# Inverse norms of queries and keys on the GpSimd engine with its power operation, and each sine product as one VectorE operation: a 12-layer local-attention and feed-forward kernel

## The reference

```python
def l2norm(t):
    return t / jnp.maximum(jnp.linalg.norm(t, axis=-1, keepdims=True), 1e-12)

def rotate_half(x):
    x1, x2 = jnp.split(x, 2, -1)
    return jnp.concatenate([-x2, x1], -1)

def attn_layer(x, Wqkv, qs, ksc, Wo):          # 16 heads of 64
    ...
    q = l2norm(q) * qs
    k = l2norm(k) * ksc
    ...
    q = q * cos * scale + rotate_half(q) * sin * scale
    k = k * cos * inv + rotate_half(k) * sin * inv
    out = local_attention(q, k, v)
    ...
    return out @ Wo
```

## Time and profile before

| | |
|---|---|
| median of 3 runs | 7130.14 us (7125.9 to 7132.31) |
| the profiled execution | 7134.42 us, span 7132.6 us |
| busy share of the span | DVE 85%, PE 83%, PEld 54%, ACT 46%, POOL 34% |
| granted TensorE clock, mean | 0.934 of full speed |
| first stack, from its first tiles to its end | about 418 to 2700 us |
| top-k attention between the stacks | about 2700 to 4800 us |
| one layer of a stack (exponential of tile 0 to the same of the next layer) | 354.8 us (958.07 to 1312.91) |
| one full tile step | 17.3 us |

### The profile page before, as it was taken

How to read it: one execution, slowest core, us unless ns; L and a number is a source line. 1 busy time by engine, 2 the same in 40 slices (tenths; PEclk the granted TensorE clock), 3 DMA queues, 4 the chain that set the end, 5 groups by cost and what they waited for, 6 DMA issues and landing times. The chain is left out here.

```text
span 7132.6 us, 149904 instructions
## 1 busy us (share of the span) xinstructions
PE 5922.3 (83%) x47404; PEld 3834.3 (54%) x47596; DVE 6041.5 (85%) x12676; ACT 3310.3 (46%) x6408; POOL 2418.6 (34%) x1391
## 2 busy tenths in 40 slices
PE   5776888888888887988988988986888888888888
PEld 2224545555555554565565566565555555555555
DVE  5988888888888885998998998996979797979797
ACT  3335656565555552222222222222656565656564
POOL 1444444434343431122122122221525253525252
PEclk7998999999999998998998998988999999999999
DMA  0002222222222210000000000000212121212121
GB/s 14 0 0 63 59 52 59 52 59 52 59 52 59 53 46 14 1 1 1 1 1 1 1 1 1 1 1 15 60 51 60 51 60 51 61 50 62 50 62 37
DMA packets 159611, 244.33 MB, mean 34 GB/s; under 512 B 36597, under 2 KB 57009, under 8 KB 157495
## 3 DMA queue, kind: packets, MB, share of 16 engines
q1 hardware_dynamic: 159158, 238.71, 13.3%
HBM read 36.20 MB, written 1.05 MB: 5 GB/s over the span
## 5 line engine op out<-in xcount | busy, mean ns | idle before, releaser
L879 POOL TENSOR_TENSOR f_rope<-f_rope,f_t 128x1024 f32<-128x1024 f32 x384 | 907.3, 2363 | 1551.9 <-DVE f_t L759 1551.9
L1315 PE MATMUL psum<-tk_kT,tk_qs 128*128 128x512 f32 (+3 forms) x4128 | 1262.4, 466 | 9.1 <-POOL tk_qs L1548 9.1
L1548 POOL TENSOR_TENSOR tk_qs<-tk_qT,tk_mix 128x1024 f32<-128x1024 f32 x258 | 497.8, 1932 | 1588.6 <-PE psum L1316 1423.9
L882 POOL TENSOR_TENSOR f_rope<-f_rope,f_rn 128x1024 f32<-128x1024 f32 x384 | 752.6, 1960 | 721.1 <-DVE f_rn L738 706.1
L1315 PEld LDWEIGHTS psum<-tk_kT,tk_qs 128*128 128x128 f32 x4128 | 756.8, 208 | 439.7 <-issue 297.6
L454 PE MATMUL psum<-f_wqkv,f_xs 128*128 128x512 f32 x1536 | 774.1, 610 | 84.9 <-DMA f_wqkv<-in_Wqkv 56.0
L1505 DVE MAX8 tk_m<-tk_work 128x8 f32<-128x528 f32 (+3 forms) x1792 | 818.6, 496 | 2.3 <-issue 1.2
L1511 DVE MATCH_REPLACE8 tk_work<-tk_m,tk_work 128x400 f32<-128x400 f32 (+3 forms) x1536 | 743.8, 491 | 0.5
L755 DVE TENSOR_TENSOR f_rope<-f_raw,f_rot 128x1024 f32<-128x1024 f32 x384 | 627.2, 1633 | 24.5 <-ACT f_raw L600 17.6
L600 ACT ACTIVATE f_raw<-psum 128x512 f32<-128x512 f32 x768 | 454.6, 595 | 247.3 <-PE psum L454 187.9
L473 PEld LDWEIGHTS psum<-ident,f_rope 128*128 128x128 f32 x3072 | 350.4, 144 | 343.9 <-ACT f_qT L600 216.5
(11 more groups left out here) (234 smaller groups left out, 10915.4 us busy)
## 6 DMA issues: line engine op xcount, KB each, us to landing
f_v<-f_v_tok SPq DMA_DIRECT2D x1152, 128.0 KB, 2.4
f_v<-f_v_tok SPq DMA_DIRECT2D x768, 64.0 KB, 2.0
f_wqkv<-in_Wqkv SPq DMA_DIRECT2D x12, 1536.0 KB, 6.6
f_wo<-in_Wo SPq DMA_DIRECT2D x12, 512.0 KB, 4.0
f_w<-in_W SPq DMA_DIRECT2D x12, 341.0 KB
f_w<-in_W SPq DMA_DIRECT2D x24, 64.0 KB
tk_wkv<-in_Wkv SPq DMA_DIRECT2D x1, 1024.0 KB, 6.0
out<-y_tok SPq DMA_DIRECT2D x4, 256.0 KB, 2.5
```

Source lines behind the costliest of these rows:

```text
L879: pool.tensor_tensor(part, part, t2[:, half, :, :], ALU.add).then_inc(s["rope_added"], 1)
L882: pool.tensor_tensor(part, part, rn[:, H * half:H * (half + 1)].unsqueeze(2).to_broadcast([P, H, DH]), ALU.mult).then_inc(s["add_done"], 1)
L1315: pe.matmul(psum[:, j, 0:n], qs[:, j, c, :], kT[:, c, 0:n], start=(c == 0), stop=False, skip_group_check=True)
L1548: pool.tensor_tensor(qs[:, j, :, :], qT[:, :, P * t:P * (t + 1)], mix[:, :, heads(p, j)].to_broadcast([P, PAIRS, P]), ALU.mult).then_inc(s ...
```

## The change

- `newton` and the table `magic` are gone from DVE. A function `inverse_norm` on POOL makes `rn` in six operations on 128x32 elements: the maximum with 1e-24, the power -0.5 (`ALU.pow`, with a tile that holds -0.5), and one polishing step of four operations. It is placed between the sum (L879, now L872) and the multiplication (L882, now L877) of half 0, and waits for both reductions of the tile.
- DVE's sum and reciprocal of the softmax follow the reductions directly. Before the first reduction DVE waits for the inverse norms of the tile before (`rn_ready`).
- The two sine operations of a half become one of 1024 columns, which reads `raw` through a view with the two halves of each head in reversed order.

```diff
@@ -714,31 +713,6 @@
                 for sem, n in ((s["rot_done"], 2), (s["ss_done"], 2), (s["sub_done"], 1), (s["on_done"], 1)):
                     dve.sem_inc(sem, n)
 
-                def newton(g, between):
-
-                    at = [0]
-
-                    def link(ins):
-                        at[0] += 1
-                        ins.then_inc(s["newton"], 1)
-                        if at[0] in between:
-                            between[at[0]]()
-
-                        wait_alone(dve, s["newton"], NEWTON * g + at[0], s["scrap"]) if at[0] == 2 else dve.wait_ge(s["newton"], 1 + NEWTON * g + at[0])
-
-                    x, h, y, z = (nt[:, n, :] for n in range(4))
-                    link(dve.tensor_scalar(x, ss[:, :], 1e-24, None, ALU.max))
-                    link(dve.tensor_scalar(h.bitcast(U32), x.bitcast(U32), 1, 0xFFFFFFFF, ALU.logical_shift_right, ALU.bitwise_xor))
-                    link(dve.tensor_tensor(y.bitcast(U32), h.bitcast(U32), k.magic[:, :], ALU.add))
-                    for n in range(3):
-                        link(dve.scalar_tensor_tensor(z, y, -0.5, y, ALU.mult, ALU.mult))
-                        link(dve.tensor_tensor(h, z, x, ALU.mult))
-                        if n == 2:
-                            dve.wait_ge(s["add_done"], 1 + 2 * g + 2)
-                            dve.scalar_tensor_tensor(rn[:, :], h, 1.5, y, ALU.add, ALU.mult).then_inc(s["rn_ready"], 1)
-                        else:
-                            link(dve.scalar_tensor_tensor(y, h, 1.5, y, ALU.add, ALU.mult))
-
                 def shifted(L, b, j, t):
 
                     late = not isinstance(t, int) or t >= 2
@@ -754,10 +728,10 @@
                     cos = rot[:, half, j, :].unsqueeze(1).to_broadcast([P, H, DH])
                     dve.tensor_tensor(rope[:, j % 2, half, :, :], raw[:, half, :, :], cos, ALU.mult)
                     dve.wait_ge(s["add_done"], 1 + 2 * g + half + 1)
-                    for q in range(2):
-                        sin = rot[:, 2 + half, j, hd * q:hd * (q + 1)].unsqueeze(1).to_broadcast([P, H, hd])
-                        last = dve.tensor_tensor(t2[:, half, :, hd * q:hd * (q + 1)], raw[:, half, :, hd * (1 - q):hd * (2 - q)], sin, ALU.mult)
-                    last.then_inc(s["rot_done"], 1)
+                    sin = rot[:, 2 + half, j, :].rearrange("p (q e) -> p q e", q=2).unsqueeze(1).to_broadcast([P, H, 2, hd])
+                    swapped = raw[:, half, :, :].rearrange("p h (q e) -> p h q e", q=2)[:, :, ::-1, :]
+                    dve.tensor_tensor(t2[:, half, :, :].rearrange("p h (q e) -> p h q e", q=2), swapped, sin,
+                                      ALU.mult).then_inc(s["rot_done"], 1)
 
                 def step(L, b, j, kk):
                     g0 = LT * L + kk
@@ -784,10 +758,10 @@
                         rotate(g0, j, 0)
                         for half in range(2):
                             dve.wait_ge(s["sq_done"], 1 + 2 * g0 + half + 1)
+                            if half == 0:
+                                dve.wait_ge(s["rn_ready"], 1 + g0)
                             dve.tensor_reduce(ss[:, H * half:H * (half + 1)], sq[:, half, :, :], AX_X, ALU.add).then_inc(s["ss_done"], 1)
-                        dve.wait_ge(s["ss_done"], 1 + 2 * g0 + 2 + 2)
-                        newton(g0, {2: den_sum, 4: den_recip} if on(kk, 2) else {})
-                    elif on(kk, 2):
+                    if on(kk, 2):
                         den_sum()
                         den_recip()
                     if on(kk, 2):
@@ -860,6 +834,25 @@
 
             @block.gpsimd
             def _(pool):
+                def inverse_norm(g):
+
+                    x, y, z, h = (nt[:, n, :] for n in range(4))
+                    n0 = 1 + NEWTON * g
+                    wait_alone(pool, s["ss_done"], 2 * g + 2 + 2, s["scrap"])
+                    pool.tensor_scalar(x, ss[:, :], 1e-24, None, ALU.max).then_inc(s["newton"], 1)
+                    pool.wait_ge(s["newton"], n0 + 1)
+                    pool.tensor_tensor(y, x, minus_half[:, :], ALU.pow).then_inc(s["newton"], 1)
+                    pool.wait_ge(s["newton"], n0 + 2)
+                    pool.tensor_tensor(z, y, y, ALU.mult).then_inc(s["newton"], 1)
+                    pool.wait_ge(s["newton"], n0 + 3)
+                    pool.tensor_tensor(h, z, x, ALU.mult).then_inc(s["newton"], 1)
+                    wait_alone(pool, s["newton"], NEWTON * g + 4, s["scrap"])
+                    pool.tensor_scalar(z, h, -0.5, 1.5, ALU.mult, ALU.add).then_inc(s["newton"], 1)
+                    pool.wait_ge(s["newton"], n0 + 5)
+                    pool.tensor_tensor(rn[:, :], y, z, ALU.mult).then_inc(s["rn_ready"], 1)
+
+                pool.memset(minus_half[:, :], -0.5).then_inc(s["halved"], 1)
+                pool.wait_ge(s["halved"], 1 + 1)
                 pool.sem_inc(s["wo_done"], 1)
                 pool.sem_inc(s["out_full"], 1)
                 pool.sem_inc(s["add_done"], 2)
@@ -877,6 +870,8 @@
                             pool.wait_ge(s["rot_done"], 1 + 2 * g0 + half + 1 + 2)
                             part = rope[:, j % 2, half, :, :]
                             pool.tensor_tensor(part, part, t2[:, half, :, :], ALU.add).then_inc(s["rope_added"], 1)
+                            if half == 0:
+                                inverse_norm(g0)
                             pool.wait_ge(s["rope_added"], 1 + 2 * g0 + half + 1)
                             pool.wait_ge(s["rn_ready"], 1 + g0 + 1)
                             pool.tensor_tensor(part, part, rn[:, H * half:H * (half + 1)].unsqueeze(2).to_broadcast([P, H, DH]),
```

More of the change, by code:

```diff
@@ L36 @@
 REMOVED = -3.4e38
-MAGIC = 0x5F3759DF
-NEWTON = 11
+NEWTON = 5
 HCH = [(0, 128), (128, 128), (256, 85)]
@@ L249, in _ @@
             dve.memset(k.XB[:, :, :], 0.0)
-            dve.memset(k.magic[:, :], MAGIC + 1)
             dve.wait_ge(s["built"], 1 + 1)
@@ L337, in ffn_stack @@
         s = names(ctx, phase, nc, *LN_SEMS, "wqkv_in", "wo_in", "w12_in", "tabled", "zeroed", "xs_ready", "proj_full", "proj_evac", "v_in_even", "v_in_odd",
-                  "sq_done", "ss_done", "newton", "rn_ready", "rope_added", "rot_done", "add_done", "t_full",
+                  "sq_done", "ss_done", "newton", "halved", "rn_ready", "rope_added", "rot_done", "add_done", "t_full",
                   "t_evac", "scores", "top", "sub_done", "exp_done", "summed", "rden_done", "pv_done", "on_done",
@@ L355, in ffn_stack @@
         rn = sb("rn", [P, 2 * H])
+        minus_half = sb("minus_half", [P, 2 * H])
         rope = sb("rope", [P, 2, 2, H, DH])
@@ L1587, in build @@
         k.mask_f, k.causal, k.band = sb("mask_f", [P, P]), sb("causal", [P, P], BF16), sb("band", [P, 2, 8, 2 * WIN], BF16)
-        k.eps, k.one, k.magic = sb("eps", [P, 1]), sb("one", [P, 1]), sb("magic", [P, 2 * H], U32)
+        k.eps, k.one = sb("eps", [P, 1]), sb("one", [P, 1])
         k.b1, k.b2 = sb("b1", [P, DEPTH, 2, 3]), sb("b2", [P, DEPTH])
```

## The result

The changed kernel takes 7308.56 us (median of 4 runs, 7306.23 to 7314.81) against 7131.23 us (4 runs): ratio 1.0249, 95% interval 1.0236 to 1.0262. That is 177 us more where 160 less were forecast.

The account below looks back on a forecast made before the run. The loop was taken as bound by DVE, with PE and ACT close behind. Gains of 8.8 + 0.4 + 1.6 + 2.5 = 13.3 us a layer, times 12, gave 160 us: 6970 us forecast, range 6905 to 7135.

Parts of the forecast that it names:

- The power, p: Duration of POOL's power operation on 32 columns in the inverse norm: taken as 0.6 us, range 0.23 to 2.37.
- rival 1: Slow power delays POOL's multiplication of half 0 and, past 1.3 us, DVE's subtraction; slower past about 2.3 us; chance 0.19.
- POOL has 8 us to spare in a step: POOL's idle time per steady step, 8 us, would hide a slow power if the port were not locked.
- the lock named above: Port pair shared by DVE and POOL, claimed to be held exclusively for a whole instruction; L755's 1.92 us cited as evidence.
- The steady step: One tile step in mid-layer: 0.91 us gained in three of four, 0.18 in the fourth; steps of 16.4 and 17.1 us.
- The start of a layer: Tile 0's exponential waits 4.02 us for DVE; gain taken as 2.5 us, ends 1.3 and 5.4.
- The twelve full steps: The full steps of one layer, nine gaining 0.91 us and three 0.18: 8.8 us per layer.
- the drain: End of a layer, where tile 14's exponential waits 3.51 us: DVE's subtraction comes earlier, gaining 1.6 us.
- rival 3: Layer starts gain all: 5.4 us and up to 2 more per layer, giving 6912 us; chance 0.1.
- The alternating queue at the port: At layer start POOL's six short operations and DVE's 1.2-us operations alternate, ending the inverse norm about 1 to 2 us later.
- The sine product: On DVE, one 1024-column product of 1.22 us replaces two taking 1.28: 0.06 us less per half, reversed view free.
- DVE's new wait: DVE's wait for the earlier tile's inverse norms costs nothing, since they are made nearly a step earlier.

Follow-up runs that it names:

- the run with a multiplication: The changed kernel with the power replaced by a multiplication on the same tiles, so inverse norms are not computed: 6912.08 us, ratio 0.9693 to the kernel before.
- the stand-in: The changed kernel with the power replaced by two plain 1024-column products on scratch and a 32-column multiplication: 7365.77 us, ratio 1.0319 to the kernel before.
- the altered order: The changed kernel with POOL doing both sums, then the inverse norm, then both multiplications: 8241.21 us, ratio 1.1557 to the kernel before.

## Why the prediction was wrong

- **The step that failed: "The power, p, is in no row ... I take p = 0.6, and keep 0.23 and 2.37 for the range."** It is 5.46 us. The factor 6 to 7 came from a reciprocal on another engine; POOL's own factor is 158 ns a column against 2.16 for a sum, 73. The upper end was worse: what 1024 columns of a sum cost is a duration from the trace, but nothing connects it with the power, so it bounded nothing. The estimate of 0.3 us from the page on GpSimd (the Trainium skill, GPSIMD Engine Reference, "Elementwise — side-by-side cycle accounting") was further off still: 158 ns are some 190 cycles at the 1.2 GHz that the page gives, not 12. The chance of slower, 0.19, was too small for a price without a row.
- **"Past p = 1.3 each microsecond delays L755 through the port and so the subtraction, 1 to 1"** (rival 1, with its turn at 2.3 us). The rival had the right sign, but not the mechanism. Its own prices (14 us a layer at 2.37, then 1 to 1 in 15 steps a layer) give 7694 us at p = 5.46, against 7309 measured. A short power does cost through the port, but at another operation (L733, by 1.17 us a step at 1.67) and not 1 to 1. A long one fills POOL's step, with the turn near 4.4. "POOL has 8 us to spare in a step" stood in the text, but I did not add it up: 9.0 + 1.8 for the five small operations and their gaps (the inverse norm in the run with a multiplication takes 1098.09 to 1100.10, 2.0 with p = 0.25) + p reaches 17.3 at p = 6.5, and 2 us of waiting at the port and for DVE's product, worked out only after the runs, bring that to 4.5.
- **"Without the lock named above a slow power would stay hidden."** I rested this on the Trainium skill (SBUF — State Buffer, "SBUF: two separate sides"), by which a GpSimd operation holds the shared port pair for the whole instruction. For sums and products the traces agree (2.84 us for DVE's L730 beside the stand-in). For the power they do not: DVE's products of two SBUF tensors take 1.22 us beside it. And it did not stay hidden, for the reason above.
- **The steady step apart from p was right.** With a cheap operation in the power's place the times within the step agree to 0.3 us and the steps to 0.1 us.
- **The start of a layer** was put at 2.5 us between 1.3 and 5.4. In the run without a power the stretch from the last exponential of a layer to the second of the next is 95.30 + 16.94 us, where it was 97.92 + 19.72 in the kernel before: 5.4 us gained, where 2.5 + 0.4 stood in the sum. The twelve full steps gained 10.0 us (207.91 to 197.92; forecast 8.8) and the drain 1.6 (forecast 1.6). That is the 17.0 us by which this layer became shorter (354.84 to 337.88). The mean of the layers is 18.5 (222 / 12); they do not gain alike, the first layer 21.9 (356.58 to 334.65), and why was not followed. The time, 6912 us, is that which rival 3 gave, but this is luck: the start of a layer gave 5.4 us and not 7.4 + 0.4, the steps more than forecast. The alternating queue at the port that I had walked through was too pessimistic at the start, or faster matmuls made up for it; that was not separated.
- **The drain** was right: the wait of the exponential of tile 14 went from 3.51 to 2.02 us in that run, and the step before it from 17.35 to 15.70.
- **The sine product** was right: 23 us forecast, 27 measured, with the interval 17 to 37.
- **That DVE's new wait costs nothing** stayed true: DVE's first reduction waits for ACT's square alone in the changed kernel; in the altered order another wait of that kind, for the buffer `t2`, cost 8.7 us a step.

## What to carry to other kernels

A price that no row shows is not bounded by a row of something else: before work is moved to an engine, time the new operation by itself, or give the outcome "it is ten times dearer" its full chance. Then add up the receiving engine's whole step, moved work and waits for the port included, and compare it with the step's length; here an engine at half load was full after one operation of 5 us in a 17-us step. Ask also what the operations behind the new one will now run beside: with a power of 1.7 us POOL had time left, and the kernel still lost 100 us to collisions. What takes load off the binding engine and puts none on another (a polishing round fewer, one operation for two) gave 2.3% here, at the price of slightly less exact norms, where the move lost 2.5%.

## What the runs showed of the hardware that I had not expected

- POOL's power on two SBUF inputs costs 158 ns per column and 0.40 us, against 2.16 ns per column for a sum: 5.46 us for 128x32.
- The power waits for the port at its start (6.42 us when issued just behind a VectorE product, 5.46 otherwise), but VectorE's products on two SBUF tensors run beside it at their full 1.22 us.
- Two engines that wait for the port take turns operation by operation: 0.18 us of lateness made a multiplication 2.79 us long and the product behind it 2.93. Such a pair in most tiles goes with 101 us in all; a power 1.3 us longer gave the same time, with the collision at the products of half 0 instead.
